# Four states of a channel on neighbouring partitions, replicated with 32 outer rows; B and C double buffered; the first norm's result kept in DRAM

## The reference, cut to what matters

```python
def mamba(h, ...):                       # inner 256 channels, 16 states, rank 64, 4 taps
    x, z = split(h @ W_in.T)
    x = silu(causal_conv(x, conv_w) + conv_b)
    dt, B, C = split(x @ Wx.T)           # 64, 16, 16
    dt = softplus(dt @ Wdt.T + bdt)      # (tokens, 256)
    dA  = exp(dt[..., None] * -exp(A_log))        # (tokens, 256, 16)
    dBx = (dt * x)[..., None] * B[:, None, :]     # (tokens, 256, 16)
    state = dA_t * state + dBx_t                  # over tokens, one after the other
    y = sum_over_states(state * C_t) + x * D
    return (y * silu(z)) @ W_out.T

x1  = layernorm(x + mamba(x) + flip(mamba_rev(flip(x))))
xn  = layernorm(x1) * ln_gamma + ln_beta
w_q = clip(round(w / (mean|w| + eps)), -1, 1);  gamma = max|xn|
out = layernorm(x1 + (clip(xn * 128 / gamma) @ w_q) * (gamma * mean|w| / 128))
```

## Time and profile before

| | |
|---|---|
| median of 3 runs | 1044.81 us (1042.97 to 1050.16) |
| the profiled execution | 1041.62 us |
| its span | 1039.8 us |
| DVE busy | 906.6 us, 87% |
| POOL busy | 856.6 us, 82% |
| PE busy | 669.3 us, 64% |
| ACT busy | 598.6 us, 58% |
| DMA, share of 16 engines | 38.1% |

### The profile page before, as it was taken

One profiled execution on the slowest core, in us unless ns is written; L12 is line 12 of the kernel. 1 busy time (PEld: TensorE's weight loads), 2 busy tenths in 40 slices (PEclk: granted clock), 3 DMA queues, 4 the chain that ended last, 5 costly groups with the idle time before them and its releaser, 6 DMA issues. The chain is left out here.

```text
span 1039.8 us, 9415 instructions
## 1 busy us (share of the span) xinstructions
PE 669.3 (64%) x2124; PEld 221.2 (21%) x2124; DVE 906.6 (87%) x1004; ACT 598.6 (58%) x974; POOL 856.6 (82%) x384
## 2 busy tenths in 40 slices
PE   6537637777667666677567666778576676556432
PEld 3212102222212212122112121213121221012122
DVE  2268769999999999999999999999999999999936
ACT  3436544756476665665476766665575756554414
POOL 0169579999798999999799999997998999997602
PEclk9858867788888788788789889688779788666656
DMA  2344404444343424443453424443433424441002
GB/s 57 99 129 127 143 22 118 140 110 137 95 130 94 130 83 127 133 124 114 114 142 82 137 74 134 127 129 109 120 99 97 142 75 135 124 133 49 0 1 81
DMA packets 84071, 109.56 MB, mean 105 GB/s; under 512 B 21040, under 2 KB 34352, under 8 KB 84016
## 3 DMA queue, kind: packets, MB, share of 16 engines
q1 hardware_dynamic: 84016, 108.97, 38.1%
HBM read 38.65 MB, written 3.15 MB: 40 GB/s over the span
## 5 line engine op out<-in xcount | busy, mean ns | idle before, releaser
L440 POOL TENSOR_TENSOR dbx<-dtx_rep,b_rep 128x1024 f32<-128x1024 f32 x256 | 612.6, 2417 | 63.7 <-DMA dtx_rep<-dtx 45.6
L629 ACT ACTIVATE da_ps<-dt_rep,neg_a 128x512 f32<-128x512 f32 x512 | 350.4, 688 | 339.2 <-DVE hs L892 335.1
L892 DVE TENSOR_TENSOR_SCAN hs<-da_ps,dbx 128x512 f32<-128x512 f32 x256 | 296.9, 1207 | 46.2 <-POOL dbx L440 19.8
L892 DVE TENSOR_TENSOR_SCAN hs<-da_ps,carry,dbx 128x512 f32<-128x512 f32 x256 | 312.2, 1267 | 26.8 <-issue 14.3
L1142 PE MATMUL y_ps<-ch,stack 128*32 128x512 f32 x1024 | 178.4, 775 | 209.7 <-DVE ch L782 135.5
L450 POOL TENSOR_TENSOR ch<-hs,c_rep 128x1024 f32<-128x1024 f32 x96 | 226.1, 2356 | 28.6 <-issue 13.9
L782 DVE TENSOR_TENSOR ch<-hs,c_ps 128x1024 f32<-128x1024 f32 x160 | 191.4, 1196 | 0.0
L1133 PE MATMUL c_ps<-x_dbl,select 128*128 128x512 f32 x256 | 179.5, 789 | 0.0
L1085 PE MATMUL pre<-h_t,w_conv 128*128 128x512 f32 x256 | 120.5, 614 | 7.6 <-ACT xs L530 6.4
L1142 PEld LDWEIGHTS y_ps<-ch,stack 128*32 128x32 f32 x1024 | 24.8, 120 | 324.2 <-issue 220.2
L1133 PEld LDWEIGHTS c_ps<-x_dbl,select 128*128 128x128 f32 x256 | 47.0, 229 | 146.2 <-issue 133.8
(11 more groups left out here) (125 smaller groups left out, 507.7 us busy)
## 6 DMA issues: line engine op xcount, KB each, us to landing
dt_rep<-dt SPq DMA_DIRECT2D x512, 64.0 KB, 2.1
dtx_rep<-dtx SPq DMA_DIRECT2D x512, 64.0 KB, 2.6
b_rep<-bc_rows SPq DMA_DIRECT2D x64, 256.0 KB
c_rep<-bc_rows SPq DMA_DIRECT2D x64, 256.0 KB
h_in<-in_L_attn_hidden_states SPq DMA_DIRECT2D x4, 512.0 KB, 5.6
h_res<-in_L_attn_hidden_states SPq DMA_DIRECT2D x4, 512.0 KB, 6.7
out<-hs SPq DMA_DIRECT2D x4, 512.0 KB, 2.9
bc_rows<-x_dbl SPq DMA_DIRECT2D x16, 64.0 KB, 4.7
```

The source lines that it names most:

```text
L440: nc.gpsimd.tensor_tensor(dbx[:, n % RING], dtx_rep[:, r], b_rep[:, k, :].unsqueeze(1).to_broadcast([P, 2, CHUNK]), ALU.mult).then_inc(dbx ...
L629: nc.scalar.activation(da_ps[:, half % DA_BANKS, :], dt_rep[:, r, e, :], ACT.Exp, scale=neg_a[:, half_of(unit), 2 * (unit % 2) + e, g, k:k ...
L892: nc.vector.tensor_tensor_scan(in_scan_order(hs[:, n % RING, e, :], s), in_scan_order(da_ps[:, (2 * n + e) % DA_BANKS, :], s), in_scan_ord ...
```

## The change

Partition 4 d + i now holds channel d and state i: the four states of a channel are neighbours. `dt` and `dtx` are interleaved in one tensor `step`, and a slot's half is replicated by one transfer whose source is [32 partitions, 4 times the same, 1024] and whose destination is [128 partitions, 1024]. B and C rows are interleaved in DRAM, a transfer carries both for four states, with 32 repeats outermost, and the replicated rows have two buffers. `dt` is now sent with `dtx`, after both are there. `x1` is no longer in SBUF: `xn` is stored to DRAM after each norm but the last, the second norm writes into `resid`, and all tiles but the last four are loaded back after the last scan, into the place of `dbx`. Constants follow the new order of partitions: `stack`, `select` and a new `spread` and `state_of` for the decays' constant. The sum of |w| and the all-reduce are done in the prologue.

```diff
-        dt = sb("dt", [P, DT, CHUNK])
-        dtx = sb("dtx", [P, DT, CHUNK])
+        step = sb("step", [P, DT, 2, CHUNK])
+        dt, dtx = step[:, :, 0, :], step[:, :, 1, :]
...
-        dt_rep = sb("dt_rep", [P, 2 * DT, 2, CHUNK])
-        dtx_rep = sb("dtx_rep", [P, 2 * DT, 2, CHUNK])
-        b_rep = sb("b_rep", [P, STATES // QUAD, CHUNK])
-        c_rep = sb("c_rep", [P, STATES // QUAD, CHUNK])
+        step_rep = sb("step_rep", [P, 2 * DT, 2, 2, CHUNK])
+        dt_rep, dtx_rep = step_rep[:, :, :, 0, :], step_rep[:, :, :, 1, :]
+        bc_rep = sb("bc_rep", [P, 2, STATES // QUAD, 2, CHUNK])
+        b_rep, c_rep = bc_rep[:, :, :, 0, :], bc_rep[:, :, :, 1, :]
...
-        x1 = sb("x1", [P, TILES, P])
+        spread = resid[:]
+        a_rows = xn[:, 0:2, :].rearrange("p t m -> p (t m)").rearrange("p (k i) -> p k i", i=QUAD)
+        x1_last = dbx[:, :, :, :].rearrange("p a b t -> p (a b t)").rearrange("p (j m) -> p j m", m=P)
+        x1_rows = nc.dram_tensor("x1_rows", (P, TILES, P), f32).ap()
-        bc_rows = nc.dram_tensor("bc_rows", (NG, 2 * STATES, CHUNK), f32).ap()
+        bc_rows = nc.dram_tensor("bc_rows", (NG, STATES, 2, CHUNK), f32).ap()
...
             load_conv(FWD, conv_in)
+            sp.dma_start(w_raw[:], w_ffn).then_inc(w_raw_in, 16)
...
-                sp.dma_start(bc_rows[s], x_dbl[0:2 * STATES, s % 2, :]).then_inc(rows_stored, 16)
+                sp.dma_start(bc_rows[s].rearrange("n c t -> c n t"), x_dbl[0:2 * STATES, s % 2, :]).then_inc(rows_stored, 16)
-            def load_dt(b, s, r):   ...
-            def load_dtx(b, s, r):  ...
+            def load_step(b, s, r):
                 group = NG * b + s
                 sp.wait_ge(dtx_ready, group + 1)
                 if group:
+                    sp.wait_ge(da_ready, 2 * (UNITS * (group - 1) + last_of_slot(r) + 1))
                     sp.wait_ge(dbx_ready, UNITS * (group - 1) + last_of_slot(r) + 1)
                 for e in range(2):
                     k = BLOCK * (2 * (r % 2) + e)
-                    for i in range(QUAD):
-                        sp.dma_start(dtx_rep[BLOCK * i:BLOCK * (i + 1), r, e, :], dtx[k:k + BLOCK, r // 2, :]).then_inc(dtx_in[r], 16)
+                    rows = step[k:k + BLOCK, r // 2].rearrange("p c t -> p (c t)")
+                    sp.dma_start(step_rep[:, r, e].rearrange("p c t -> p (c t)"),
+                                 rows.unsqueeze(1).to_broadcast([BLOCK, QUAD, 2 * CHUNK])).then_inc(step_in[r], 16)
-            def load_b(b, s, k):    ...
-            def load_c(b, s, k):    ...
+            def load_bc(b, s, k):
                 group = NG * b + s
                 sp.wait_ge(rows_stored, 16 * (group + 1))
+                if group >= 2:
+                    sp.wait_ge(dbx_ready, UNITS * (group - 1))
+                    sp.wait_ge(ch_pool, pool_c(*before(b, s)))
+                rows = bc_rows[s, QUAD * k:QUAD * (k + 1)].rearrange("n c t -> n (c t)")
+                sp.dma_start(bc_rep[:, s % 2, k].rearrange("p c t -> p (c t)"),
+                             rows.unsqueeze(0).to_broadcast([BLOCK, QUAD, 2 * CHUNK])).then_inc(bc_in[s % 2][k], 16)
+            def store_x1(b, h_e):
+                e = 2 * b + h_e
+                sp.wait_ge(x1_ready, TT * (e + 1))
+                sp.dma_start(x1_rows[:, x1_tiles(e), :], xn[:]).then_inc(x1_stored, 16)
...
                     if group:
-                        load_dt(b, s, 2)
-                        load_dt(b, s, 3)
-                        load_c(b, s, 3)
+                        load_step(b, s, 2)
+                        load_step(b, s, 3)
...
+                    if not (last and s == NG - 1):
+                        store_rows(*nxt)
+                        for k in range(STATES // QUAD):
+                            load_bc(*nxt, k)
+                        load_step(*nxt, 0)
+                        load_step(*nxt, 1)
+                    if s == NG - 1:
+                        store_x1(b, 0)
+                    if s == 0 and not first:
+                        store_x1(b - 1, 1)
 
             store_rows(0, 0)
-            load_b(0, 0, 0)
-            load_dt(0, 0, 0)
-            load_dtx(0, 0, 0)
...
+            load_bc(0, 0, 0)
+            load_bc(0, 0, 1)
+            load_step(0, 0, 0)
+            load_step(0, 0, 1)
             for k in range(2, STATES // QUAD):
-                load_b(0, 0, k)
+                load_bc(0, 0, k)
             for r in (2, 3):
-                load_dt(0, 0, r)
-                load_dtx(0, 0, r)
+                load_step(0, 0, r)
             batches(sp, batch)
+            sp.wait_ge(scanned, 2 * UNITS * NG * BATCH)
+            sp.wait_ge(x1_stored, 16 * (2 * BATCH - 1))
+            kept = slice(0, TILES - 2 * TT), slice(TILES - TT, TILES)
+            for tiles in kept:
+                sp.dma_start(x1_last[:, tiles, :], x1_rows[:, tiles, :]).then_inc(x1_in, 16)
...
-                        if first and s == 1 and n == 0:
-                            pool.wait_ge(w_sum, 1)
-                            nc.gpsimd.partition_all_reduce(tiny[:, 1:2], tiny[:, 0:1], P, REDUCE.add).then_inc(w_sum_all, 1)
...
+            pool.wait_ge(w_sum, 1)
+            nc.gpsimd.partition_all_reduce(tiny[:, 1:2], tiny[:, 0:1], P, REDUCE.add).then_inc(w_sum_all, 1)
             for n in range(B_AHEAD):
                 times_b(0, 0, n)
...
 # ACT
                         for k in range(2 * DT):
-                            act.wait_ge(dt_in[k], 2 * QUAD * 16 * q)
+                            act.wait_ge(step_in[k], 2 * 16 * q)
                         act.wait_ge(dtx_ready, q)
...
                 act.wait_ge(bias1_ready, e + 1)
+                if e:
+                    act.wait_ge(x1_stored, 16 * e)
...
-                act.wait_ge(x1_kept, e + 1)
+                act.wait_ge(x1_ready, TT * (e + 1))
...
-            def keep_x1(b_e, h_e): ...
...
 # DVE
+            dve.wait_ge(w_raw_in, 16)
+            nc.vector.tensor_reduce(tiny[:, 0:1], w_raw[:], X, ALU.add, apply_absolute_value=True).then_inc(w_sum, 1)
...
+            def own_states():
+                dve.wait_ge(a_ps, 1)
+                chained(nc.vector.tensor_tensor(a_rows, da_ps[:, 0, 0:QUAD * 2 * DT * STATES].rearrange("p (k i) -> p k i", i=QUAD),
+                                                state_of[:].unsqueeze(1).to_broadcast([P, 2 * DT * STATES, QUAD]), ALU.mult))
+                nc.vector.tensor_reduce(neg_a[:].rearrange("p a j g k -> p (a j g k)"), a_rows, X, ALU.add).then_inc(a_log_ready, 1)
...
                     dve.wait_ge(o_ps, e + 1)
+                    if e:
+                        dve.wait_ge(xn_ps, e)
...
             copy_weights()
+            own_states()
             prepare(0, 0, "dtx")
...
+                    last = j == 2 * BATCH - 2
+                    if not last:
+                        dve.wait_ge(x1_in, 16 * 2)
+                    kept = xn[:] if last else x1_last[:, t, :]
```

More of the change, by code:

```diff
@@ L1102, in replicate_a @@
                 pe.wait_ge(dt_cols_in, 16 * 6)
[L1103 to L1109 removed]
+                for a in range(DT):
+                    for j in range(QUAD):
+                        at = (QUAD * a + j) * 2 * STATES
+                        ins = nc.tensor.matmul(da_ps[:, 0, at:at + 2 * STATES], spread[:, j, :], a_log[:, :, a, :], start=True, stop=True)
                 ins.then_inc(a_ps, 1)
```

134 lines of the change are left out of this document (37 added, 97 removed).

## The result

| | before | after |
|---|---|---|
| median of 4 runs each | 1043.89 us (1042.94 to 1050.16) | 1012.19 us (1010.03 to 1014.17) |
| ratio | | 0.9684 [0.9639, 0.9728] |
| profiled execution; span | 1041.62; 1039.8 us | 1014.17; 1012.0 us |

The medians lie 31.7 us apart, the forecast said 33.9 (1011 us, range 1002 to 1028). The two spans lie only 27.8 apart: the profiled execution of the changed kernel was the slowest of its four. What follows divides the 27.8.

A forecast was written before the change was run, and what follows sets the result against it. DVE, busy 87%, was taken as the bound, with recoverable gaps at the start and in one-time waits. From the 1044.8 us median, -19.6 (replication) and -14.3 (all-reduce) sum to -33.9, giving 1011 us, range 1002 to 1028.

The forecast's parts named there:

- Replication of the step, -19.6: Group 0: fewer, larger step transfers at 298 GB/s let unit 5 and group 1 start earlier, saving 19.6 us.
- bound of 10 to 13 us for half the rate: Group 0: if the 512 KB transfers move at 150 GB/s, the replication gains only 10 to 13 us.
- lengthening towards 5 us: Sign on SP's queue that the forecast is wrong: issues of 512 KB transfers growing from about 0.6 towards 5 us.
- rival 1: Transfers miss the rate and DMA becomes the bound, POOL waiting for slot 1 in every group: about 1190 us, 6%.
- group length still 58.2: Sign in the loop that the forecast is right: a group still takes 58.2 us.
- Fewer issues, 2.5 us in place of 20.2: SP's queue before group 0: issuing the first two slots takes 4 x 0.63 = 2.5 us, not 32 x 0.63 = 20.2.
- B and C with 32 outer rows: Start of group 0: B and C rows no longer take 2.87 us per 256 KB at 91 GB/s; no separate term.
- The prologue at 0 to 1 us: Prologue: added DVE work fits inside the 7.95 us DVE waits for ACT before dtx; 0, at worst 1 us.
- The all-reduce, -14.3: Moved from group 1 to the prologue, its 17.9 us hide in POOL's idle start, removing DVE's 14.3 us wait.
- First norm in DRAM, 0: Closings and tail: store and 1.8 MB load back cost 0; the load has 28 us for 6 to 8.
- Rival 2: Only one part pays: start's gain falls to 5 us or the all-reduce's cost returns in group 0; 1018 to 1030, 12%.
- Rival 3: Gain given back in the loop: DVE waits for ACT instead of POOL, 25 to 30 us back; 1036 to 1041, 6%.

The follow-up runs named there:

- e5: Changed kernel with each replication's source every fourth partition instead of 32 neighbours, constants not reordered, so channels go to wrong places: 1009.22 us, 0.9649 of the kernel before.
- e6: Changed kernel with each 512 KB replication transfer cut into four of 128 KB, one for each state: 1011.09 us, 0.9687 of the kernel before.
- e7: Changed kernel with B and C rows read with four outer rows, as before the change, states going to other partitions: 1019.56 us, 0.9753 of the kernel before.
- e1: The changed kernel run and profiled once more with no edit: 1014.81 us, 0.971 of the kernel before.
- e3: Kernel before the change with only the sum of |w|, its load and the all-reduce moved to the prologue: 1030.38 us, 0.9865 of the kernel before.
- e2: Changed kernel with the all-reduce put back in the loop, at unit 0 of group 1: 1022.28 us, 0.9781 of the kernel before.
- e4: Changed kernel with B rows and C rows stored by two transfers in place of one: 1012.01 us, 0.9687 of the kernel before.
- e12: Changed kernel with one buffer for the replicated B and C rows in place of two, with the waits this needs: 1013.37 us, 0.9696 of the kernel before.
- e8: Changed kernel with each 512 KB step replication reading 4 neighbouring partitions 32 times, data going to wrong places: 2913.35 us, 2.7901 of the kernel before.

## Why the prediction was right, and where it was off

*What bounds the kernel.* Right: the middle gave nothing. Groups 2 to 15 took 795.9 us against 798.6; the 2.6 are DVE's waits before the sums into `resid` (10.9 us in groups 1 to 15 before, 8.4 after), which no step of the prediction had. No run tests them.

*Replication of the step, -19.6.* The mechanism was right, the size 2.8 too large; dtx to group 1 fell by 16.8 us, counted from dtx and so without the prologue. What was mis-sized is the rate: 298 GB/s were read off a window in which the engines were half busy and in part with transfers of another kind, and the transfers got 191 in the window that is nearly all theirs. The trace before has a window with no transfers but the old replications, also from 32 neighbouring partitions:

```profile
36.00:40.00 4.00, 1.69 (x3) 0.92 (x4) 0.00 (x0) 3.96 (x4) 0.00 (x0) 0.86 0.44 109
```

It gives 109 / 0.44 = 248 GB/s, nearer but still too high: what half-busy engines move, scaled up, isn't what full ones move. So POOL could use slot 1 at 48.58, 15.5 us behind dtx (33.10), where the prediction has 40, 11.6 behind it. e5 isolates this: same bytes, shapes and issues, source partitions apart, and dtx to group 1 falls to 63.7, under the 66.0 that the prediction has (28.4 to 94.4), with unit 1 14.2 behind dtx, just as forecast (28.4 to 42.6; 17.9 in the changed kernel). Its bound of 10 to 13 us for half the rate was not reached. The sentence set beside this step, on the Trainium skill's page SBUF — State Buffer (Door 1: The DMA port swizzle), was the better guide: by the page 32 neighbouring partitions tend to about 218 GB/s, the window shows 183 moved, 191 at full use, and e5 exceeds that with partitions that, by the page's map, reach all 16 ports. The delay estimated there, 1 to 2 us, was worked out too low: 2.1 MB at 218 GB/s take 2.6 us more than at 298, and unit 1 came 3.7 late against dtx.

One of the prediction's signs came by halves: of the four issues of 512 KB before group 0 (7.80 us) two took 0.57 and 0.60 us, the third 3.96 and the fourth 2.54. The row of eight at 77.72 is no price of an issue: its 24.47 us hold SP's waits for buffers as well, and e5, at about twice the rate, has 23.21 there. The prediction had "lengthening towards 5 us" as a sign of rival 1; 3.96 came, and yet POOL waits for no transfer in the loop. Another sign, "group length still 58.2", forgot that the 58.2 hold the stall of 14.3: without it they are 57.2, and 57.1 were measured.

*Fewer issues, 2.5 us in place of 20.2.* Half right. e6 issues 16 for two slots (10.12 us) and loses nothing, though its rate is another too. No run sends the old transfers in the new order, so how much of the 16.8 us is the order on SP and how much the number of issues isn't shown.

*B and C with 32 outer rows.* The prediction had it within the same term and gave it no price. e7 gives one: 5 to 7 us by the medians, 8.3 by dtx to group 1 (77.2 less 68.9). That is about half of what the first group gained.

*The prologue at 0 to 1 us.* dtx came 4.7 late in the profiled execution, and at 28.9 in e1. The granted clock tells the two apart: where it was 1.00 from 24 to 28 us, dtx lay at 28.4 to 29.9 (six executions of the table, both kernels among them); where it was 0.50, at 31.0 to 33.4 (seven). But the clock isn't all of it. PE's timelines of the changed kernel and of e1, the same first eight products and the same four behind them:

```profile
9.55 5.24 PE L1080 MATMUL pre<-h_t,w_conv 128*128 128x512 f32 x8
22.36 3.17 PE L1092 MATMUL pre<-xs,w_mix_t 128*128 128x512 f32 x4 [1.80 <-DVE wx_rev_t L723]
```

```profile
9.52 4.03 PE L1080 MATMUL pre<-h_t,w_conv 128*128 128x512 f32 x8
21.11 1.95 PE L1092 MATMUL pre<-xs,w_mix_t 128*128 128x512 f32 x4 [1.80 <-DVE wx_rev_t L723]
```

From the start of the four products to dtx it is 7.8 us in every execution of the table at 1.00, and 10.4 to 10.8 in every one at 0.50: that is the clock's share, 2.9 of the 4.7. The other 1.8 were lost before it fell. The row of the four starts at 22.36, in the kernel before at 20.57, and 1.6 of that is the eight products, which took 3.67 there (and 3.60 to 5.58 in the other runs) while the granted clock read 1.00; why is open. The 0.5 by which e1's dtx is late (28.91 against 28.37) stands in the same place, the four start 0.5 late, so that the added DVE work behind them cost nothing. In both executions PE had stood idle for 1.80 us before the four; in one its clock fell. Neither of the two executions of the old order (before, e3) had it; with two, whether the change makes the fall likelier stays open.

*The all-reduce, -14.3.* Right, and shown alone: e3 gains 14.4 us by the medians, 13.5 in group 1. It starts at 9.86 (9.6 was forecast) and POOL's next instruction waits for its transfer, not for the 6.9 us. The 0.8 that is missing fits the quantising, whose three instructions took 5.06 us before and now take 6.73, one of them 6.27 alone. POOL was busy beside them both times. DVE and POOL before:

```profile
144.10 0.52 DVE L757 TENSOR_SCALAR w_q<-w_raw,tiny 128x128 f32<-128x128 f32 x1
144.66 2.27 DVE L758 TENSOR_SCALAR w_q<-w_q 128x128 f32<-128x128 f32 x1
146.95 2.27 DVE L759 TENSOR_SCALAR w_q<-w_q 128x128 f32<-128x128 f32 x1
```

```profile
142.19 4.65 POOL L440 TENSOR_TENSOR dbx<-dtx_rep,b_rep 128x1024 f32<-128x1024 f32 x2
146.80 2.34 POOL L450 TENSOR_TENSOR ch<-hs,c_rep 128x1024 f32<-128x1024 f32 x1
```

Each ends 0.1 us behind the end of one of POOL's instructions; the 6.27 run past the ends of two and to that of the third (123.88). In eight of the nine executions with the reduction early and the quantising in the loop, one of the three took 6.26 to 6.29 us. In the ninth, e1, they took 2.06, 2.28 and 0.23, and group 1 was 15.7 us shorter than before. Putting the reduction back (e2) costs 11.9 to 14.1 of group 1 but only 7.5 by the medians. The rest of that difference isn't explained: by the marks e2 reaches group 2 11.7 after e1, and its rest is 2.5 shorter.

*The store.* 0, as forecast; slower by 1.3 us than two stores and hidden (e4).

*Double buffering, 0.* Right (e12). *Scans unchanged.* Right: 1191, 1206 and 1229 ns at the minimum, the median and the maximum, for the earlier trace rows, with the engines' share at a half. *First norm in DRAM, 0.* Right: 986.73 waits for nothing and the tail is 0.4 longer. It was not undone by itself.

*The sum.* -33.9 forecast, -27.8 by the marks: 4.7 lost in the prologue (2.9 to its clock), 2.8 to the rate, 0.8 to the quantising, 0.4 in the tail, 2.6 won in the loop. The medians, over executions with other prologues, show -31.7.

*The rivals.* Rival 1 didn't happen. e8 shows that it is real when the source is 4 neighbouring partitions read out 32 times. Rival 2 (only one part pays): each part pays without the other, 22.5 us in e2 and 14.4 in e3. Together they are 6.9 more than the 30.0 that the changed kernel gained on the same chip (e1). The 5.3 that its profiled execution lost in one `step` product are of that size; whether its other executions lost them too isn't shown. Rival 3: DVE's waits for ACT in groups 1 to 15 are 25.3 us in 21 in both kernels; nothing was given back. In group 0 they are 4.8 where they were 5.7: the wait of 3.32 in the earlier trace rows is now 2.39, and the two others, 1.60 and 0.8, stay.

## What to carry to other kernels

A rate for a new transfer must come from a stretch in which the engines are full of such transfers, from the same source partitions. Scaled up from half-busy engines it was 298 or 248 GB/s; measured it was 191. With shapes, bytes and issues alike the replication ran at 183 GB/s from 32 neighbouring partitions and at 344 from every fourth (36 to 44 us). Whether that matters is set by the first group, which has no work ahead of it to hide in; the later groups hid all but the slowest (e8). One-time work that stalls an engine in the loop is best sought in the profile as a wait that happens once, and moved to where that engine waits anyway.
